# A wait between accumulating stores, and expert weights fetched one tile later, in the last stage of a two-layer transformer kernel

## The reference

```python
def _L1_ffn_ref(hidden_states, Wr, br, W1, W2):
    x = hidden_states.reshape(-1, h)
    route = jax.nn.sigmoid(x @ Wr + br)
    max_prob = jnp.max(route, axis=1, keepdims=True)
    max_ind = jnp.argmax(route, axis=1)
    out = jnp.zeros_like(x)
    for e in range(n_experts):                       # 8 experts
        mask = (max_ind == e)[:, None].astype(x.dtype)
        y = jax.nn.gelu(x @ W1[e], approximate=False) @ W2[e]
        out = out + mask * y
    out = out * max_prob
    return out.reshape(b, s, h)
...
h = _layernorm(x, axis=-1) * (1 + cb) + sb
x = x + gb * _L1_ffn_ref(h, L1_ffn_Wr, L1_ffn_br, L1_ffn_W1, L1_ffn_W2)
return x
```

## Time and profile before

| what | value |
|---|---|
| timed runs | 1805.25, 1807.93, 1808.53 us |
| the profiled execution, its own time | 1808.53 us |
| its span (first to last event) | 1806.8 us |
| PE busy | 1588.0 us (88%) |
| DVE, ACT, POOL busy | 1144.6, 943.5, 1087.8 us |
| mean granted clock of PE | 0.931 of full speed |
| last stage, first weight fetch to end of the span | 1564.5 to 1806.8 us |

### The profile page before, as it was taken

The page is one execution under the profiler, slowest core; times in us unless marked ns, Lnnn a source line. Parts: engine busy times, 40 slices in busy tenths (PEclk is TensorE's granted clock), DMA queues, the critical chain, the costliest instruction groups (busy, mean ns, idle before and its releaser), DMA issues.

```text
span 1806.8 us, 38384 instructions
## 1 busy us (share of the span) xinstructions
PE 1588.0 (88%) x13772; PEld 1181.1 (65%) x13772; DVE 1144.6 (63%) x1769; ACT 943.5 (52%) x2333; POOL 1087.8 (60%) x933
## 2 busy tenths in 40 slices
PE   6699999987999999999999657888886866699997
PEld 5456656665888888888888532334443425599997
DVE  7778898875334333443444386999999998533332
ACT  5678888842444444444544266444443425455553
POOL 4647777631333333333444399899997995466664
PEclk9899999985999999999999866999998988599999
DMA  6003434226332333323443360011111245388885
GB/s 211 24 27 123 131 115 123 88 96 246 98 97 86 103 106 103 93 87 106 147 141 88 112 209 1 1 30 30 42 32 34 88 134 182 131 252 257 259 260 138
DMA packets 136000, 209.26 MB, mean 116 GB/s; under 512 B 45248, under 2 KB 96336, under 8 KB 130704
## 3 DMA queue, kind: packets, MB, share of 16 engines
q1 hardware_dynamic: 114752, 132.22, 23.0%
q0 software_dynamic: 21072, 74.60, 13.9%
HBM read 139.00 MB, written 67.76 MB: 114 GB/s over the span
## 4 chain that ended last, share of the span: by engine, by line
PE 64%; POOL 12%; DVE 10%; issue 5%; DMA 3%; ACT 2%; POOLq 0%; SPq 0%; DVEq 0%; ACTq 0%
PE ps L759 61%; POOL BIG L2338 9%; DVE BIG L1330 5%; DVE BIG L1850 2%; DMA BIG<-HB,BIG 2%; PE ps L876 1%; ACT BIG L1898 1%; POOL BIG L2545 1%; PE ps L1047 1%; DMA HB<-BIG 1%; POOL X L2338 1%; PE ps L1116 0%; DVE BIG L1543 0%; POOL out L2486 0%; DVE BIG L1828 0%
## 5 line engine op out<-in xcount | busy, mean ns | idle before, releaser
L759 PE MATMUL ps<-BIG 128*128 128x256 f16 (+9 forms) x11304 | 1289.8, 287 | 112.9 <-DVE BIG L1828 46.1
L759 PEld LDWEIGHTS ps<-BIG 128*128 128x128 f16 (+3 forms) x11304 | 974.3, 101 | 388.9 <-issue 70.7
L2338 POOL TENSOR_TENSOR BIG<-BIG 128x256 f16<-128x256 f32 (+6 forms) x547 | 734.4, 1381 | 426.6 <-ACT BIG L1898 404.9
L1898 ACT ACTIVATE BIG<-BIG 128x512 f16<-128x512 f32 (+3 forms) x543 | 328.6, 659 | 210.0 <-DVE BIG L1330 177.9
L1330 DVE TENSOR_TENSOR BIG<-BIG 128x512 f16<-128x512 f32 (+10 forms) x343 | 273.8, 808 | 235.4 <-ACT BIG L1898 212.4
L1898 ACT ACTIVATE BIG<-ps 128x64 f32<-128x64 f32 (+6 forms) x756 | 265.7, 417 | 216.8 <-PE ps L759 173.7
L1330 DVE TENSOR_TENSOR BIG<-ps,BIG 128x512 f32<-128x512 f32 (+2 forms) x389 | 278.1, 776 | 14.5 <-PE ps L759 13.1
L1330 DVE TENSOR_TENSOR BIG<-BIG,ps 128x512 f32<-128x512 f32 (+2 forms) x181 | 112.8, 623 | 249.2 <-PE ps L759 244.5
L1850 DVE TENSOR_REDUCE BIG<-BIG 128x160 f32<-128x2560 f32 x64 | 182.2, 2847 | 0.0
L2476 POOL DMA_INDIRECT BIG<-HB,BIG x109 | 111.2, 1020 | 70.5 <-DVE BIG L1330 39.2
L2488 POOL DMA_INDIRECT YT<-BIG x70 | 70.2, 1003 | 102.7 <-ACT BIG L1898 102.0
(11 more groups left out here) (143 smaller groups left out, 956.6 us busy)
## 6 DMA issues: line engine op xcount, KB each, us to landing
WD<-BIG SPq DMA_DIRECT2D x80, 256.0 KB
BIG<-in_v SPq DMA_DIRECT2D x32, 512.0 KB
BIG<-in_w SPq DMA_DIRECT2D x24, 512.0 KB
BIG<-WD SPq DMA_DIRECT2D x32, 384.0 KB, 7.3
HB<-BIG SPq DMA_DIRECT2D x64, 128.0 KB, 2.5
WG<-BIG SPq DMA_DIRECT2D x32, 256.0 KB
BIG<-YT SPq DMA_DIRECT2D x16, 512.0 KB, 5.1
BIG<-WD SPq DMA_DIRECT2D x16, 512.0 KB, 5.2
```

The source lines that it names most:

```text
L759: return e.matmul(o, lhsT, rhs, start=start, stop=stop, skip_group_check=True)
L1898: return e.activation(o, i, ACT.Copy)
L2338: return e.tensor_tensor(o, a, b, op)
```

## The change

```diff
                 if l:

                     pool.wait_ge(st_x, 16 * NT)
+                    if t:
+                        pool.wait_ge(st_y[(t - 1) % 2], slot_base[l]["y"][(t - 1) % 2] + 16 * ((t - 1) // 2 + 1))
                     e.indirect_dma_start(m_.YT, to, m_.YO[t % 2], None, compute_op=ALU.add).then_inc(st_y[t % 2], 16)
                 else:
                     e.indirect_dma_start(m_.YT, to, m_.YO[t % 2], None).then_inc(st_y[t % 2], 16)
@@
                 fetch(1, 1)
                 fetch_weights(1)
                 fetch(1, 2)
-                fetch_weights(2)
                 for j in range(NS):
                     if j + 3 < NS:
                         fetch(1, j + 3)
-                        fetch_weights(j + 3)
+                    if j + 2 < NS:
+                        fetch_weights(j + 2)
                     if j:
                         put(1, j - 1)
                 put(1, NS - 1)
```

## The result

The changed kernel takes 1826.31 us (median of 4 timed runs, 1823.78 to 1830.06) where the kernel before takes 1807.91 us. The ratio is 1.0106, with a 95% interval of 1.0086 to 1.0127. It is 18.4 us slower, by much more than the 3.2 us of the forecast, and lies over the end of its range (1819 us). Rival 2 had the sign and the nearest size (+11 us), but not, as it turned out, the reason.

The account below looks back on a forecast made before the run. The prediction took PE to bound the last stage with an almost full DMA queue beside it; 2.3 us for later weights plus 0.9 us at the last store gave 3.2 us, a median of 1811.1 us, range 1806 to 1819 us.

Parts of the forecast that it names:

- Rival 2: Last stage: weights become the beat once their latency is over 6.1 us on average; +11 us, 1819 us; chance 0.22.
- What bounds the kernel: Last stage: PE bounds it, busy 187.81 of 190 us, with the DMA queue almost full beside it at 0.89.
- Part A, nothing for tiles 1 to 37: Stores waiting for the store before: the queue doesn't run dry behind a held store, so 0 us, bounds 0 to 3.
- The end: Last store waits for the data of tile 37's store plus 0.3 us: 0.9 us, bounds 0.6 and 1.3 us.
- Part B: Weights fetched one tile later: some land after PE's upward product wants them; 2.3 us, bounds nothing and 7 us.
- The start: Start of the last stage: weights of tiles 2 and 4 are issued later but land in time; counted as nothing.
- The sum: Whole kernel: + 2.3 + 0.9 = 3.2 us on the profiled execution, forecast as a median of 1811.1 us.
- Rival 1: Last stage: only the wait at the last store is paid, later weights are free; 1808.8 us; chance 0.28.
- Rival 3: Last stage: the 16 engines run less apart, most of PE's lost 3.8 us goes; - 2.9 us, 1805.0 us; chance 0.10.
- The rule weighed: Weight fetch: fixed 2.0 us plus bytes at 436 GB/s, 4.4 us for 1 MB; holds for an empty queue only.

Follow-up runs that it names:

- A alone: Kernel before, with each last-stage store also waiting for the landing of the store before it, weights fetched as early as before: 1825.5 us, ratio 1.0095.
- A with early rows: Kernel before, with each store waiting for the landing of the store before it and rows fetched one tile earlier: 1820.7 us, ratio 1.0069.
- every second store: Kernel before, with only odd tiles' stores waiting for the landing of the store before: 1819.8 us, ratio 1.0069.
- the weights first: The changed kernel, with weights issued ahead of the rows and rows fetched one tile earlier: 1810.9 us, ratio 1.0023 to the kernel before.
- part B alone: Kernel before, with weights fetched one tile later and stores waiting for nothing new: 1816.3 us, ratio 1.0053.

## Why the prediction was wrong, point by point

**What bounds the kernel: right.** PE and the DMA queue side by side, the rows just in time. The run with rows one tile earlier shows the waits for rows and their end.

**Part A, nothing for tiles 1 to 37: this is the step that failed.** Its argument was that a store is late only because the queue is full, and that 1.25 MB behind it keep the queue busy meanwhile. It looked at one held store, and closed no loop. It also took a store as landed too early: with its last packet + 1.1 us for the landing, 31 of the 38 stores of the kernel before come before the landing of the one ahead of them, by 31 us together, where the prediction read a third of the stores and 12 us. Closed, the loop reads: store, rows and weights are issued in 4.4 us; the weights need L; the next store's data lie behind them for about 0.9 us; 1.1 us later the store after that can start. Two beats are 6.4 us + L. With the traced L this gives 6.2 us for A alone (traced 6.21), 6.1 us for A with early rows (6.19), 6.2 us for every second store (6.10). In the change the weight issue takes 1.34 us more often than 0.95, so 6.6 + 5.5 = 12.1 us give 6.05 (6.07). For PE's 5.55 us L would have to be under 4.7 us, and it is that only with half of the bytes (3.4). The formula was made after the result, and the run with A alone was forecast from it with an L of 5.5 us and a beat of 5.95; both came out higher (6.0 and 6.21), and the cost lay over its range. The runs with early rows, with every second store, and with the weights first came later, and their beats came out. Their costs in time lay just below the range in the first case and at its low end in the other two.

The reason that nothing is lost since the queue doesn't run dry fell with it: the DMA share went from 0.89 to 0.82, with 1.5 us of little data in the beat shown.

**The end: right in kind, mis-sized.** 0.9 us were forecast, by a notice of 0.3 us after the last data; the distance grew by 1.84 us in the change and 1.87 in the run with this wait alone. The 0.3 us were the idle time between two issues on POOL, which is no measure of how long a landing needs to be seen. That error is small at the end, but 1.1 instead of 0.3 us stands in each pass of the chain: over 19 passes of two beats, 0.8 us each are 15 us, an estimate.

**Part B: mechanism right, size wrong.** Slots are late, and PE waits for weights in their place. The prediction read 7 of 36 slots as late, some 7 us in sum, refused to add them up since the queue would catch up while PE waits, and took 2.3 us. Its readings were too kind. It took the end of the data from the rate by stretch and called it the landing. By the last packets, the hard slot of 1743.32 ends at 1752.0 and not 1751.4, the easy one of 1653.88 at 1659.8 and not 1659.1, and the first fetch needs 4.3 and not 3.9 us. And PE starts later than the last packet: eight of its ten waits in the run with part B alone end 0.4 to 0.6 us after it. With the last packets and 0.4 us, 15 of the 36 slots are late by more than 0.3 us, 17 us in sum. 9.1 us were measured, so some half of it is caught up; the forecast had two thirds of a sum caught up that was less than half as large. The lateness was mis-sized more than the catching up. A reason why it isn't more: each issue waits in POOL's program behind a store, each store for DVE's result, and that for PE, so a wait of PE moves the next issues as well. L stayed at 5.8 us in that run. In the change itself this cost doesn't show beside that of part A.

**The start: right.** From the first weight issue to the first store it is 24.0 us where it was 24.65.

**The sum.** Part A for the tiles 0 forecast and all but the end of its 18.3 us measured; part B 2.3 against 9.1, but hidden under A; the end 0.9 against 1.9.

**Rival 2** named a beat of 5.97 us from three beats and an L of 7. The beat was 6.07, yet L was 5.5, and A alone reaches it without late weights. Its number was near for another reason. Rival 1 is out: part A costs 18.3 us and part B 9.1, each alone. Rival 3's mechanism is out with parts A and B. Its waits for rows can be removed, and bring 1.4 us.

**The rule weighed.** The first fetch in the changed kernel again needs 4.3 us from the end of its issue to its last packet on an empty queue. What I didn't draw from the same section of the Trainium skill ("DMA: Bandwidth & Descriptors", "Anatomy of one DMA") is that most of the fixed time lies between the last byte and the semaphore, and is longest for a write to HBM. The traces agree in kind: about 1.1 us from the last packet of a store to HBM until POOL starts the next store, accumulating or plain, and mostly 0.4 to 0.6 us from the last packet of a weight fetch into SBUF until PE starts. The two waits are on different engines, so not all of the difference need be the memory's.

**The long weight issues.** In the changed kernel a weight issue takes 1.34 us more often than 0.95 (mean 1.19 against 0.99 us). The traces of all 13 kernels tell what goes with it. From 1590 us on, 157 of 441 weight issues took over 1.2 us. Each of these 157 began while one of DVE's operations of L1330 (SBUF to SBUF) was under way with 0.40 to 0.65 us left, and ended 0.80 to 0.86 us after that operation. The operation and the issue seem to hold each other up. The issue of 1721.42 above is one; DVE's row beside it:

```profile
1721.26 0.69 DVE L1330 TENSOR_TENSOR BIG<-BIG 128x512 f16<-128x512 f32 x1 [1.00 <-ACT BIG L1898]
```

The operation ends at 1721.95, the issue at 1722.76. Of the 284 shorter issues none began with so much left of one, but for 28 that began at most 0.05 us after an operation did: these stayed at 0.98 us, and the operation took 0.76 us and not 0.69. So where DVE's work falls sets up to 0.4 us of each pass of the loop. That is read from the traces; no run moved DVE's operation alone.

What stays open: why part B costs nothing beside part A, and what early rows alone do for part B.

## What to carry to other kernels

A wait between two transfers of one queue must be costed as a loop: go from the held instruction through all that is issued behind it, through the queue, and back to the wait, and compare the whole with the beat; what stands ahead of the awaited transfer on the queue counts in full. Where issues hang on the consumer's own results, late transfers are caught up only in part: of some 17 us read from the trace of before, 9 were paid. And the order of issues in the loop is worth as much as the depth: with the 1 MB fetch ahead of the small one and rows a tile earlier, the same wait cost 3 to 4 us and not 18, and without the wait this order (1804.9 us) was one of the two fastest of those that compute the whole result, 0.15% under the kernel before, level with early rows alone.

## What was not expected of the hardware

- A store to HBM is seen as landed no sooner than 1.08 us after its last data packet, by the start of the next store. PE, when it waits, mostly starts 0.4 to 0.6 us after the last packet of a weight fetch into SBUF.
- An accumulating indirect store of 128 KB took 1.62 us to issue and ran at up to 164 GB/s in half a microsecond; a plain one took 0.97 us and ran at 254 GB/s. With part A the difference is worth 17 us (1825.5 against 1808.8 us).
- In the beat shown of the changed kernel a 1 MB gather, issued until 1722.76, reaches 377 GB/s only at 1724.5, with 74 to 147 GB/s in between.
- All 157 weight issues of over 1.2 us began during an operation of DVE and ended 0.80 to 0.86 us after it.
